# A fused two-layer model on one core: both choices' output rows side by side in memory, and the routing table's pieces shared out anew

## The reference, cut to what matters

```python
for _ in range(2):                               # LOOPS
    x = rmsnorm(z, norm_w)                       # T=4096 tokens, D=256
    combine = combine_weights(x, w_macro, w_micro)   # [T, 8], two non-zero entries a token
    h = silu(einsum('td,efd->tef', x, w1))       # 8 experts, F=512
    y = einsum('tef,edf->ted', h, w2)
    z = z + einsum('ted,te->td', y, combine)
```

## Time and profile before

| | before |
|---|---|
| median of 3 runs | 3186.93 us (3181.68 to 3194.24) |
| profiled execution, its own time | 3191.04 us |
| its span, first to last instruction | 3189.2 us |
| TensorE busy (PE) | 2637.8 us, 83% |
| VectorE busy (DVE) | 1919.7 us, 60% |
| ScalarE busy (ACT) | 1592.5 us, 50% |
| GpSimd busy (POOL) | 1076.0 us, 34% |
| mean granted TensorE clock | 0.914 |

### The profile page before, as it was taken

The page is one execution under the profiler, slowest core; times in us unless marked ns, Lnnn a source line. Parts: engine busy times, 40 slices in busy tenths (PEclk is TensorE's granted clock), DMA queues, the critical chain, the costliest instruction groups (busy, mean ns, idle before and its releaser), DMA issues. The chain is left out here.

```text
span 3189.2 us, 61231 instructions
## 1 busy us (share of the span) xinstructions
PE 2637.8 (83%) x16220; PEld 1567.4 (49%) x16221; DVE 1919.7 (60%) x4520; ACT 1592.5 (50%) x2490; POOL 1076.0 (34%) x1744
## 2 busy tenths in 40 slices
PE   8689999999997679985699876888888888648887
PEld 5333333333333568864588743444444444424554
DVE  4478888888884843336433373677776663756641
ACT  3267777777776643333334363666666663402112
POOL 1424111111112565543555464332223312503333
PEclk9699999999999879995699987999999996869999
DMA  4500101010102512215022184111111103603321
GB/s 168 190 21 14 27 13 27 13 27 13 27 7 74 149 37 70 67 54 155 29 70 69 55 276 146 25 27 27 27 27 27 27 10 104 231 20 106 97 86 63
DMA packets 275407, 215.29 MB, mean 68 GB/s; under 512 B 186364, under 2 KB 247296, under 8 KB 274499
## 3 DMA queue, kind: packets, MB, share of 16 engines
q1 hardware_dynamic: 245060, 136.40, 15.0%
q0 software_dynamic: 17728, 52.20, 5.2%
q10 hardware_dynamic: 12480, 25.17, 2.2%
HBM read 129.26 MB, written 85.72 MB: 67 GB/s over the span
## 5 line engine op out<-in xcount | busy, mean ns | idle before, releaser
L390 DVE TENSOR_REDUCE att_mparts<-att_S 128x2 f32<-128x1024 f32 x640 | 777.3, 1225 | 172.0 <-DVEq L386 168.4
L350 ACT ACTIVATE l_z<-att_S 128x1024 f32<-128x1024 f32 x512 | 517.7, 1024 | 215.6 <-ACTq L357 215.4
L266 PE MATMUL att_S<-att_qT,att_kT 64*128 64x512 f32 (+3 forms) x1792 | 431.0, 473 | 49.6 <-PEq L261 48.3
L254 PE MATMUL att_S<-att_kT,att_qT 64*128 64x512 f32 (+3 forms) x1792 | 392.5, 432 | 74.8 <-PEq L248 64.6
L350 ACT ACTIVATE att_room<-att_S 128x1024 f32<-128x1024 f32 (+3 forms) x384 | 318.4, 831 | 218.9 <-ACTq L357 216.8
L266 PEld LDWEIGHTS att_S<-att_qT,att_kT 64*128 64x128 f32 x1792 | 175.5, 185 | 476.3 <-issue 464.8
L282 PE MATMUL att_OP<-l_z 128*32 128x512 f32 x2048 | 274.5, 608 | 0.9 <-PEq L276 0.7
L254 PEld LDWEIGHTS att_S<-att_kT,att_qT 64*128 64x128 f32 x1792 | 189.1, 191 | 174.0 <-issue 167.6
L396 DVE CUSTOM_DVE_ANT_0 att_unused<-att_S,att_mask 128x128 f32<-128x128 f32 (+3 forms) x512 | 228.4, 488 | 74.1 <-DVEq L386 72.4
L183 POOL COPY l_z<-l_z 128x256 f32<-128x256 f32 x32 | 12.7, 398 | 633.9 <-POOLq L182 633.9
L1103 POOL DMA_INDIRECT experts_xs<-scaled,ffn_source x142 | 138.8, 978 | 196.5 <-PEq L1134 156.5
(11 more groups left out here) (309 smaller groups left out, 5144.6 us busy)
## 6 DMA issues: line engine op xcount, KB each, us to landing
qkv<-qkv_y ACTq DMA_DIRECT2D x32, 384.0 KB
l_z<-qkv SPq DMA_DIRECT2D x48, 256.0 KB, 3.5
qkv<-qkv_y SPq DMA_DIRECT2D x32, 384.0 KB, 3.4
att_room<-qkv SPq DMA_DIRECT2D x48, 256.0 KB
rows<-post_rows SPq DMA_DIRECT2D x32, 384.0 KB, 3.0
ffn_w<-in_w ACTq DMA_DIRECT2D x12, 1024.0 KB
ffn_w<-in_w SPq DMA_DIRECT2D x4, 2048.0 KB
post_at<-ao SPq DMA_DIRECT2D x64, 128.0 KB, 3.1
```

What stands on the lines that cost most here:

```text
L254: mm=pe.matmul(S[:,b,h,at:at+n],qT[r,s,qt*128:qt*128+128],kT[r,s,half*512:half*512+n],start=True,stop=True)
L266: mm=pe.matmul(S[:,b,h,f:512],kT[r,s,kt*128:kt*128+128],qT[r,s,c*512+f:c*512+512],start=True,stop=not diag)
L350: nc.scalar.activation(pr[:,n%4,:,f:512],S[:,ring["e",n],:,f:512],ACT.Exp,scale=exp_scale).then_inc(s_free[ring["e",n]],1)
L390: nc.vector.tensor_reduce(mparts[:,s,:,2*qt+half],S[:,b,:,0:width(qt,half)],AX.X,ALU.max).then_inc(end,1)
```

## The change

The row of `mixed` for choice s of a token becomes 2*token+s, so that both rows of a token lie beside each other, and each of the two loads takes one run of 2 KB for each token. The targets are worked out differently: `IX` times -4 plus 1, times its sign flag, plus twice `IX` minus 2. That is one VectorE operation more (`back`), and `source` is the result shifted right by one.

In the routing table ScalarE makes six pieces of a chunk instead of five, VectorE makes one itself in the form that GpSimd uses (behind `in_row`), and GpSimd makes one instead of three. TensorE takes VectorE's piece first, without a wait of its own since `row_ready` now comes behind that piece, then GpSimd's, then ScalarE's six. `number` moves into the memory of `ge`.

```diff
@@ rms_logits, SyncE (and in the same way combine_qkv, line 1239)
-sp.dma_start(rows[:,n%R],y2_d.rearrange("(s n) c -> n s c",s=2)[n*128:n*128+128]).then_inc(rows_loaded[n%R],16)
+sp.dma_start(rows[:,n%R].rearrange("p s d -> p (s d)"),y2_d[2*n*128:2*n*128+256].rearrange("(n s) c -> n (s c)",s=2)).then_inc(rows_loaded[n%R],16)
@@ route
-Q=2*NT; PER_CHUNK=8; SCALED=5; CHUNKS=Q//PER_CHUNK
+Q=2*NT; PER_CHUNK=8; SCALED=6; DIRECT=7; CHUNKS=Q//PER_CHUNK
-number=m.sb("number",[128,2,SLOTS0]); ...
+number=ge[:,1:3]; ...
@@ route, GpSimd
-for i in range(SCALED,PER_CHUNK):
+for i in range(DIRECT,PER_CHUNK):
@@ route, TensorE
-for n,i in enumerate([*range(SCALED,PER_CHUNK),*range(SCALED)]):
+for n,i in enumerate([*range(SCALED,DIRECT),*range(DIRECT,PER_CHUNK),*range(SCALED)]):
     if i<SCALED: pe.wait_ge(named_ready,1).then_inc(named_ready,-1)
-    else: pe.wait_ge(direct_ready,1).then_inc(direct_ready,-1)
+    elif i>=DIRECT: pe.wait_ge(direct_ready,1).then_inc(direct_ready,-1)
@@ route, VectorE, in the loop over the chunks
-row_made=do(V.tensor_tensor(in_row[:,c%2],marked(128,PER_CHUNK),at(rowf,c,PER_CHUNK,128),ALU.is_equal))
+V.tensor_tensor(in_row[:,c%2],marked(128,PER_CHUNK),at(rowf,c,PER_CHUNK,128),ALU.is_equal).then_inc(dve_done,1); issued+=1
+for i in range(SCALED,DIRECT):
+    at_q=PER_CHUNK*c+i
+    row_made=do(V.tensor_scalar(named[:,c%2,i,:],marks[:,0:SLOTS0],slotf[:,at_q:at_q+1],marks[:,128+at_q:129+at_q],ALU.is_equal,ALU.mult))
@@ route, VectorE, behind the table
-do(V.tensor_scalar(number[:,0],IX[:],-2.0,float(TOK),ALU.mult,ALU.add))
+do(V.tensor_scalar(number[:,0],IX[:],-4.0,1.0,ALU.mult,ALU.add))
 sign=do(V.tensor_scalar(number[:,1],IX[:],0.0,None,ALU.is_lt))
+back=do(V.tensor_scalar(ge[:,0],IX[:],2.0,-2.0,ALU.mult,ALU.add))
 after(sign); sign=tt(number[:,0],number[:,0],number[:,1],ALU.mult)
-after(sign); sign=do(V.scalar_tensor_tensor(out=numberi,in0=IX[:],scalar=-1.0,in1=number[:,0],op0=ALU.add,op1=ALU.add))
-after(sign); ts(source[:].bitcast(I32),numberi,TOK-1,None,ALU.bitwise_and)
+after(sign); sign=tt(numberi,number[:,0],ge[:,0],ALU.add)
+after(sign); ts(source[:].bitcast(I32),numberi,1,TOK-1,ALU.arith_shift_right,ALU.bitwise_and)
```

More of the change, by code:

```diff
@@ L922, in route @@
         in_row=m.sb("in_row",[128,2,PER_CHUNK,128],F32R); in_slot=m.sb("in_slot",[128,2,SCALED,SLOTS0]); named=m.sb("named",[128,2,PER_CHUNK,SLOTS0],F32R)
-        number=m.sb("number",[128,2,SLOTS0]); numberi=posi[:].rearrange("p a q -> p (a q)")[:,0:SLOTS0]
+        number=ge[:,1:3]; numberi=posi[:].rearrange("p a q -> p (a q)")[:,0:SLOTS0]
         hot_ready=m.sem("hot_ready"); named_ready=m.sem("named_ready"); direct_ready=m.sem("direct_ready"); row_ready=m.sem("row_ready")
@@ L1238, in _ @@
                         sp.wait_ge(rows_free,1).then_inc(rows_free,-1)
-                        sp.dma_start(rows[:,new%RL],y2_d.rearrange("(s n) c -> n s c",s=2)[128*new:128*new+128]).then_inc(rows_loaded[new%RL],16)
+                        sp.dma_start(rows[:,new%RL].rearrange("p s d -> p (s d)"),y2_d[2*new*128:2*new*128+256].rearrange("(n s) c -> n (s c)",s=2)).then_inc(rows_loaded[new%RL],16)
                         sp.wait_ge(x_free,1).then_inc(x_free,-1)
```

## The result

The changed kernel takes 3167.2 us (median of 9 runs, 3164.7 to 3175.8) against 3186.9 us before (9 runs, 3181.7 to 3194.2). The ratio is 0.9947, with a 95% interval of 0.9933 to 0.9960: 17 us less, between 13 and 21. The two medians themselves lie 19.7 us apart; what follows goes by the ratio. The forecast was 13.7 us less, 3173.2 us.

What follows compares the result with a forecast made beforehand. Routing was taken as bound by GpSimd's three pieces (3.2 us a chunk), the stage between the loops by load latency. Terms -12.2-1.4-0.1 = -13.7 us took the median 3186.9 to 3173.2 us, range 3165 to 3182.

Steps and rivals of the forecast that it cites:

- Routing: Both routing blocks: moving pieces off GpSimd makes TensorE the bound, -6.1 us a block, -12.2 for both.
- The steps: Routing, chunk 2 to chunk 7: five steps at 2.4 us a chunk take 12.0 us in place of 15.3, -3.3 us.
- more than I count: Rival: line 961's wait goes in full and load latency falls 0.3 us, or a later ramp shortens 1 us; 3168.9, chance 0.21.
- The start: Routing's first chunks: the second matmul can go at about 1118.8, so chunk 2 starts at about 1120.8, not 1122.02: -1.2 us.
- The end: Routing, last `in_slot` to `number`: VectorE's tail sets it, 4.44 us in place of 6.17, -1.7 us.
- The +0.1 for `back`: Routing: the additional operation `back` and its join cost 0.15 us at most, taken as +0.1 us a block.
- The rival that the port becomes the bound: Routing: VectorE stands for GpSimd's piece, a chunk costs 2.75 us and the kernel stands at 3177.9 us; chance 0.16.
- The loads between the loops: Stage between the loops: 128 runs of 2 KB replace 256 of 1 KB, saving 100 ns a load, -1.4 us.
- The scatter: Both experts stages: same count and size of rows at other addresses, so 0 change.
- The slower rival: Experts stages: scatter landings grow until GpSimd can't free `y` in time and all 142 tiles stretch; 3201 us, chance 0.04.
- The loads behind the second loop: Stage behind the second loop: loads are hidden behind TensorE, only the very first counts, -0.1 us; sign: DMA share below 1.00.
- The experts stages: Sign of being wrong: an experts stage changes by more than 1 us.

Runs made afterwards that it cites:

- early-signal kernel: Against the full change, VectorE signals TensorE as soon as a chunk's row one-hots are made, not behind the next chunk's wait for a free buffer: 3160.9 us (one run).
- e7_full_b: The whole change measured again, against the kernel before: 3169.9 us, ratio 0.9956 (0.9940 to 0.9973).
- the halves: Against the kernel before, only the new row places with 2 KB loads (3179.7 us, 1.0003), and only the new shares of routing pieces (3168.9 us, 0.9968).

## Why the prediction was right, point by point

- **Routing, -6.1 us a block.** It was -7.4, in both blocks. The mechanism is as told: GpSimd's three pieces were the bound, TensorE with its handshake is the new one, VectorE's tail sets the end (`number` starts 0.12 us behind the cast, though TensorE was done 0.19 us before it; in the early-signal kernel TensorE was done 0.43 us before it and the 0.12 us stayed). Each of the three terms was a little small. *The steps* (-3.3) gave 3.6 since a chunk takes 2.34 us and not 2.4: the idle time in front of TensorE is 0.45 us and not 0.5, the wait at line 961 being gone in full. That was the first half of the rival "more than I count". *The start* (-1.2) gave 1.9. The step that failed is the estimate that the second matmul could go at 1118.8, 3.0 us behind the first `in_slot`. It kept the first matmul where GpSimd's first piece had held it. VectorE's piece now goes first, TensorE starts 2.18 us behind `in_slot` (1117.21), and GpSimd's piece is there by then. *The end* (-1.7) gave 1.9: the cast that I took over at 0.34 us takes 0.20 now, and so does the operation ahead of it. With `number` the tail is 2.37 us behind `ge` (1132.97 to 1135.34) where the sum had 2.58. The +0.1 for `back` was nothing, as the 1.25 us from `number` to the end of `target` show.
- **The rival that the port becomes the bound** is refuted by two things. VectorE's `in_row` still takes 1.22 us beside GpSimd's piece (and 1.22 without GpSimd), and without GpSimd the step stays 2.34 us. The Trainium skill's rule (SBUF — State Buffer, "Who interferes with whom") of a lock that the first operation holds fits what GpSimd shows, 2.02 us for a piece of 0.6. What could have hurt, that GpSimd's piece is issued first and VectorE stands, did not occur in any chunk.
- **The loads between the loops, -1.4 us.** Not shown and not refuted: the nine profiles have -1.2, a load lands 0.1 us earlier, as the sum had it (and not 0.3, as the rival "more than I count" had it). The reason that I gave is wrong, though, so if the size fits, that is luck. I read from the queues that a packet costs 9.6 to 19.1 ns beside its bytes. The 3549 packets fewer should then have saved 3549*9.6 ns = 34 us of the engines' time in the 55 us window; their time went up by 21 us. The time for a byte differs between the stages by itself, 0.040 ns in the third row (109.4/2729) and 0.057 in the first. So a line through packets of three stages measures the stages; that a packet's recorded time has waiting in it is the likely reason and not shown. The Trainium skill's figure (DMA: Bandwidth & Descriptors, "Why small descriptors are slow"), which would make this term -0.5 us, can't be told from -1.4 here either.
- **The scatter, 0.** 142 scatters of 1.02 us still, and GpSimd waited for one 4 times in place of 7, 4.2 us in place of 10.8. That is no gain of the layout: the other profiles with the new places have 0.6 to 8.3 us (whole change again, layout alone), those with the old places and four buffers 2.7 and 5.2. The slower rival has nothing for it.
- **The loads behind the second loop, -0.1.** The sign named for them, a DMA share below 1.00, did not come: it is 1.01, and TensorE is busy for 20.00 of 20.00 us as before. In that stretch SyncE's queue has 4117 packets in place of 5002, for 6.58 MB and 6.52, and its share of the engines' time is 100.0% and 99.3%. So here too fewer packets took no less of the engines' recorded time. A tenth of a microsecond can't be told in the runs.
- **The experts stages.** They changed by -1.9 and +1.2 us, more than the 1 us that I named as a sign of being wrong. That sign was badly chosen: the profiles of kernels that differ in nothing there lie between 282.8 and 287.7 us. The same goes for the rest of the kernel. The stretch behind the second loop's last stage, where nothing was changed, first in the profile after and then in another profile of the very same kernel (`e7_full_b`):

```profile
1931.00:3171.00 1240.00, 986.63 (x6568) 568.95 (x6568) 736.37 (x2332) 534.71 (x820) 393.44 (x727) 0.90 0.21 61
```

```profile
1930.00:3159.00 1229.00, 974.28 (x6568) 562.68 (x6568) 736.07 (x2332) 533.41 (x820) 393.15 (x727) 0.91 0.21 62
```

Eleven us lie between them, twelve of TensorE's busy time, with the same number of matmuls and a granted clock of 0.90 and 0.91. Single profiles therefore say nothing on a few us of the whole. The tables do, since they repeat to 0.04 us; the stage between the loops does not (67.3 to 69.9 us).

- **The whole.** -14.8 for the tables, which is shown, and some -1.2 for the loads, which is not, make 16.0 us. The three measurements have 16 on average. Of the 2.3 us beyond the forecast's 13.7, routing's larger terms are 2.6. That is also why the result lies at the bound of 0.5%, with its interval on both sides.

## What to carry to other kernels

When an engine that is the bound is relieved, write down the next loop in full, with every sequencer's wait in it and not only the busy time. Do the same for the loop that an edit makes: here an earlier signal opened a ring of 2.34 us, but the wait that it put into VectorE's sequencer made one of 2.33, and only the signal given by the operation itself brought 2.13. Where a wait for loads repeats each tile while the DMA engines are not full, put more loads under way before making the loads themselves cheaper: one number gave 11 to 13 us, the merged runs about 1 at best.

## What the runs showed that I had not expected

- Merged runs of 2 KB took as many DMA microseconds for each byte as runs of 1 KB (0.057 against 0.056 ns in the halves, 0.059 against 0.057 in the whole), and still landed 0.1 us earlier.
- With four row buffers, the same load is issued by SyncE in 0.32 us with one run for each partition and in 0.36 with two.
- Small VectorE operations at the table's end are shorter once GpSimd has finished: the cast of 128x72 takes 0.20 us after the change and took 0.34 while GpSimd's late pieces were still running. The layout alone, with GpSimd's three pieces, has 0.34 again, and the kernels in which GpSimd makes one piece or none have 0.20. VectorE's large `in_row` doesn't show this (1.22 us either way).
